# Register reads without assertions, an unrolled run of tiles, and no closing drain in a fused four-layer kernel

## The reference

```python
# layer 0: each sequence takes one of 16 domain experts
idx = jnp.clip(domain_id, 0, E - 1)
Wsel = expert_W[idx]
expert_out = jnp.einsum('bsa,boa->bso', hidden, Wsel) + bsel[:, None, :]
...
# layer 3: each token takes the two likeliest of 8 experts
probs = jax.nn.softmax(h_flat @ router_w, axis=-1)
gates, idx = jax.lax.top_k(probs, TOPK)
gates = gates / gates.sum(-1, keepdims=True)
combine = jnp.zeros((N, E), h_flat.dtype).at[jnp.arange(N)[:, None], idx].add(gates)
hid = jax.nn.relu(jnp.einsum('nd,edf->nef', h_flat, exp_w1) + exp_b1)
eout = jnp.einsum('nef,efd->ned', hid, exp_w2) + exp_b2
y = jnp.einsum('ned,ne->nd', eout, combine)
return x + y.reshape(x.shape)
```

## Time and profile before

| what | value |
|---|---|
| median of 3 runs | 672.55 us (671.54 to 674.32) |
| the profiled execution, own time | 665.42 us |
| its span, first to last instruction | 663.5 us |
| TensorE busy | 580.9 us (88%), 5008 matmuls |
| VectorE, ScalarE, POOL busy | 459.8, 307.0, 221.7 us |
| granted TensorE clock, mean | 0.943 of full speed |
| expert tiles | about 404 us to the end |

### The profile page before, as it was taken

How to read it: one execution, slowest core, us unless ns; L and a number is a source line. 1 busy time by engine, 2 the same in 40 slices (tenths; PEclk the granted TensorE clock), 3 DMA queues, 4 the chain that set the end, 5 groups by cost and what they waited for, 6 DMA issues and landing times.

```text
span 663.5 us, 15716 instructions
## 1 busy us (share of the span) xinstructions
PE 580.9 (88%) x5008; PEld 418.8 (63%) x5009; DVE 459.8 (69%) x1284; ACT 307.0 (46%) x643; POOL 221.7 (33%) x137
## 2 busy tenths in 40 slices
PE   3979989899889979689976899899799999999992
PEld 1537565386665846656656368677667778787771
DVE  6756994899979798654996926877545656564651
ACT  2328357536475254644433234657563434344440
POOL 3141614048225363171530602113532313231322
PEclk9687899999989998889989899999899999999996
DMA  6994019531376332664317758863522322122220
GB/s 205 310 245 166 4 49 238 177 107 42 127 144 207 128 126 68 157 202 179 128 56 259 245 227 302 283 174 91 145 42 42 49 37 42 35 45 43 45 36 0
DMA packets 41177, 86.37 MB, mean 130 GB/s; under 512 B 7321, under 2 KB 31938, under 8 KB 37026
## 3 DMA queue, kind: packets, MB, share of 16 engines
q1 hardware_dynamic: 21248, 56.47, 24.9%
q0 software_dynamic: 8352, 16.99, 13.9%
q10 hardware_dynamic: 11522, 12.20, 6.2%
HBM read 57.10 MB, written 29.44 MB: 130 GB/s over the span
## 4 chain that ended last, share of the span: by engine, by line
PE 49%; DVE 22%; DMA 8%; ACT 8%; issue 6%; ACTq 3%; POOL 2%; SPq 1%; DVEq 0%; POOLq 0%
PE bank L1943 8%; PE bank L1752 6%; PE bank L1932 5%; DMA stage<-in_moe_w 4%; PE bank L1934 4%; PE bank L1933 4%; PE bank L1944 4%; PE bank L1716 2%; ACTq L880 2%; PE bank L1732 2%; DVE split L1024 2%; PE bank L1761 2%; ACT split L684 2%; PE bank L1668 2%; DVE sc_sum L1137 2%
## 5 line engine op out<-in xcount | busy, mean ns | idle before, releaser
L1932 PE MATMUL bank<-xs_f,w_moe 128*128 128x128 f16 x624 | 123.0, 221 | 12.2 <-ACT stage L892 6.3
L892 ACT ACTIVATE stage<-bank,cols 128x128 f32<-128x128 f32 x312 | 88.4, 375 | 78.5 <-issue 30.7
L1934 PE MATMUL bank<-xs_f,w_moe 128*128 128x128 f16 x624 | 123.1, 221 | 0.0
L1933 PE MATMUL bank<-xs_f,w_moe 128*128 128x128 f16 x624 | 122.5, 220 | 0.0
L645 POOL DMA_INDIRECT out_x<-x_kept,ids x39 | 63.2, 1621 | 167.2 <-DVE x_kept L1518 106.7
L1932 PEld LDWEIGHTS bank<-xs_f,w_moe 128*128 x624 | 61.1, 98 | 48.8 <-issue 20.5
L1943 PE MATMUL bank<-w_moe,split 128*128 x208 | 79.2, 383 | 0.5
L1024 DVE SCALAR_TENSOR_TENSOR split<-stage,split 128x2048 f16<-128x2048 f32 x16 | 41.0, 2565 | 34.7 <-ACT split L684 34.6
L1933 PEld LDWEIGHTS bank<-xs_f,w_moe 128*128 x624 | 61.4, 98 | 2.8
L1934 PEld LDWEIGHTS bank<-xs_f,w_moe 128*128 x624 | 61.1, 98 | 1.2
L557 POOL TENSOR_TENSOR w_moe<-w_moe,sc_max 128x2048 f32<-128x2048 f32 x8 | 29.0, 3621 | 97.5 <-DVE sc_max L1132 97.5
(11 more groups left out here) (274 smaller groups left out, 1194.1 us busy)
## 6 DMA issues: line engine op xcount, KB each, us to landing
stage<-in_moe_w SPq DMA_DIRECT2D x16, 1024.0 KB, 7.6
w_split<-split SPq DMA_DIRECT2D x16, 1024.0 KB, 5.0
w_moe<-w_split SPq DMA_DIRECT2D x8, 2048.0 KB, 8.8
w_moe<-in_bias POOLq DMA_DIRECT2D x8, 1024.0 KB, 9.5
xs<-dispatched ACTq DMA_DIRECT2D x41, 130.0 KB, 2.1
w_moe<-in_x_f SPq DMA_DIRECT2D x4, 512.0 KB, 7.0
w_moe<-in_x_t SPq DMA_DIRECT2D x4, 512.0 KB, 12.5
out_x<-x4b ACTq DMA_DIRECT2D x4, 512.0 KB, 3.4
```

Source lines behind the costliest of these rows:

```text
L892: ins = act.activation(h32[j][:, f, :], bank[banks + g][:, P * (f % 4):P * (f % 4) + P], ACT.Relu, bias=moe_b1[:, bass.ds(e, 1), f], scale ...
L1932: pe.matmul(o, hi, xs_f[j][:, k, :], start=(k == 0), stop=False)
L1933: pe.matmul(o, hi, xs_f[j][:, KD + k, :], start=False, stop=False)
L1934: mm = pe.matmul(o, lo, xs_f[j][:, k, :], start=False, stop=(k == KD - 1))
```

## The change

ScalarE no longer reads `tile_ei`: it reads the packed words of `turn_ei`, takes each expert by shift and mask, and reads the row numbers as before; `tile_ei` and the two conversions that wrote it go. All these reads, SP's and ScalarE's reads of the domain experts and TensorE's word reads are built without the range test and the assertion. (SP's read of the row numbers of the regions' ends, line 511, keeps them.) TensorE's tiles 14 to 37 are written out instead of looped, and it reads the word of the next turn before the last of the eight pieces of a turn's last tile, instead of after the tile; the wait for the late plan moves there with it. ScalarE's, VectorE's and POOL's loops stay. The block is built with `no_gpsimd_drain=True`, so POOL's drain at its end is left out.

```diff
--- before.py
+++ after.py
@@ -58,6 +58,7 @@
 LEFT = 2 + TURNS * STEPS
 ENTRIES = LEFT + STEPS
 DIGIT = E
+CLAMPED = "VectorE holds the numbers within their range where it writes them"
...
@@ -304,7 +305,6 @@
...
-        tile_ei = sb("tile_ei", [1, ENTRIES], I32)
...
-        block = ctx.enter_context(nc.Block())
+        block = ctx.enter_context(nc.Block(no_gpsimd_drain=True))
...
@@ -429,7 +429,8 @@
                 sp.wait_ge(dom_ready, 1)
                 sp.wait_ge(w_step.sem, w_step.of(c, 0))
                 _, chosen = nc.values_load_multi_w_load_instructions(
-                    dom_at[0:1, bass.ds(c * CB, last)], engines=[mybir.EngineType.SP], min_val=0, max_val=NDOM - 1)
+                    dom_at[0:1, bass.ds(c * CB, last)], engines=[mybir.EngineType.SP], min_val=0, max_val=NDOM - 1,
+                    skip_runtime_bounds_check_because=CLAMPED)
                 for b in range(last):
                     sp.dma_start(w_raw[:, b, :], t["exp_w"][bass.ds(chosen[b], 1), :, :].rearrange("e a o -> a (e o)")
                                  ).then_inc(w_raw_in.sem, 16)
@@ -793,7 +794,8 @@
             act.wait_ge(dom_ready, 1)
             _, chosen = nc.values_load_multi_w_load_instructions(
-                dom_at[0:1, CB // 2:CB], engines=[mybir.EngineType.Activation], min_val=0, max_val=NDOM - 1)
+                dom_at[0:1, CB // 2:CB], engines=[mybir.EngineType.Activation], min_val=0, max_val=NDOM - 1,
+                skip_runtime_bounds_check_because=CLAMPED)
...
-            def values_of(table, n, count, most):
-                _, values = nc.values_load_multi_w_load_instructions(
-                    table[0:1, bass.ds(n, count)], engines=[mybir.EngineType.Activation], min_val=0, max_val=most)
-                return values
+            def rows_at(n, count):
+                _, rows = nc.values_load_multi_w_load_instructions(
+                    tile_ri[0:1, bass.ds(n, count)], engines=[mybir.EngineType.Activation], min_val=0,
+                    max_val=E * CAP, skip_runtime_bounds_check_because=CLAMPED)
+                return rows
+            def words_of(turn, count):
+                _, words = nc.values_load_multi_w_load_instructions(
+                    turn_ei[0:1, bass.ds(turn, count)], engines=[mybir.EngineType.Activation], min_val=0,
+                    max_val=DIGIT ** (STEPS + 2) - 1, skip_runtime_bounds_check_because=CLAMPED)
+                return words
+            def expert_in(word, j):
+                return (word >> (DIGIT.bit_length() - 1) * j) & (E - 1)
...
             act.wait_ge(plan_ready, 1)
             act.wait_ge(rows_sent.sem, rows_sent.of(NCH - 1, 0))
-            row_at = values_of(tile_ri, 0, 4, E * CAP)
+            row_at = rows_at(0, 4)
             for n in range(2):
                 load_rows(row_at[n], n)
             split_high(NCH - 1, 3)
-            expert = values_of(tile_ei, 0, 4, E - 1)
+            words = words_of(0, EARLY_TURNS)
+            expert = [expert_in(words[0], n) for n in range(4)]
             act.wait_ge(w_out.sem, w_out.of(NCH, 0))
             for n in range(2):
                 act.wait_ge(weights_in, expert[n] * 16 + 16)
@@ -950,8 +965,9 @@
                 high(n, j, n % 3, 1)
             for first in range(2, EARLY - 2, 4):
-                row_at = values_of(tile_ri, first + 2, min(4, EARLY - 4 - first + 2), E * CAP)
-                expert = values_of(tile_ei, first, min(6, EARLY - first), E - 1)
+                row_at = rows_at(first + 2, min(4, EARLY - 4 - first + 2))
+                turn = first // STEPS
+                expert = [expert_in(words[turn], n - turn * STEPS) for n in range(first, min(first + 6, EARLY))]
                 for n in range(first, min(first + 4, EARLY - 2)):
...
             act.wait_ge(plan_ready, 2)
-            row_at = values_of(tile_ri, EARLY, 2, E * CAP)
-            expert = values_of(tile_ei, EARLY - 2, 4, E - 1)
+            row_at = rows_at(EARLY, 2)
+            word, = words_of(EARLY_TURNS, 1)
+            expert = [expert_in(word, n) for n in range(4)]
             for n in range(EARLY - 2, EARLY):
                 early_step(n, row_at[n + 2 - EARLY], expert[n + 4 - EARLY], expert[n + 2 - EARLY])
@@ -974,14 +991,15 @@
                 hidden(n, j, (2 * j + 2) % 4, e, 1)
             with act.Fori(EARLY_TURNS, TURNS) as i:
-                row_at = values_of(tile_ri, i * STEPS + 4, STEPS, E * CAP)
-                expert = values_of(tile_ei, i * STEPS + 2, STEPS + 2, E - 1)
+                row_at = rows_at(i * STEPS + 4, STEPS)
+                now, after = words_of(i, 2)
                 for j in range(STEPS):
-                    late_step(i * STEPS + j + 2, j % 2, row_at[j], expert[j + 2], expert[j])
-            row_at = values_of(tile_ri, LEFT + 2, TILES - LEFT, E * CAP)
-            expert = values_of(tile_ei, LEFT, TILES - LEFT + 2, E - 1)
+                    e_after = expert_in(now, j + 4) if j + 4 < STEPS + 2 else expert_in(after, j + 4 - STEPS)
+                    late_step(i * STEPS + j + 2, j % 2, row_at[j], e_after, expert_in(now, j + 2))
+            row_at = rows_at(LEFT + 2, TILES - LEFT)
+            word, = words_of(TURNS, 1)
             for n in range(LEFT, TILES):
-                late_step(n, n % 2, row_at[n - LEFT], expert[n - LEFT + 2], expert[n - LEFT])
+                late_step(n, n % 2, row_at[n - LEFT], expert_in(word, n - LEFT + 4), expert_in(word, n - LEFT + 2))
...
-                plan_step(dve.tensor_copy(tile_ei[:, 0:EARLY], tile_e[0:1, 0:EARLY]))
...
-                plan_step(dve.tensor_copy(tile_ei[:, late], tile_e[0:1, late]))
...
-            def experts_of(i, count):
-                number = pe.value_load(turn_ei[0:1, bass.ds(i, 1)], min_val=0, max_val=DIGIT ** (STEPS + 2) - 1)
-                return [(number >> (DIGIT.bit_length() - 1) * j) & (E - 1) for j in range(count)]
+            def word_of(turn):
+                return nc.values_load(turn_ei[0:1, turn:turn + 1], engines=[mybir.EngineType.PE], min_val=0,
+                                      max_val=DIGIT ** (STEPS + 2) - 1, skip_runtime_bounds_check_because=CLAMPED)
+            def expert_in(word, j):
+                return (word >> (DIGIT.bit_length() - 1) * j) & (E - 1)
...
-            def early_step(n, e, e_before):
+            def early_step(n, e, e_before, ahead=None):
+                word = None
                 tile_in(n)
                 for f in range(KF):
                     if n > 0 and f % 4 == 0:
@@ -1973,16 +1994,26 @@
                         down(n % 2, (n - 2) % 3, e_before, f)
                     if n > 0 and f == KF // 2:
                         early_turn_rows(n + 1)
-            def late_step(n, j, m, turn, e, e_before):
+                    if ahead is not None and f == KF - 2:
+                        if ahead == EARLY_TURNS:
+                            pe.wait_ge(plan_ready, 2)
+                        word = word_of(ahead)
+                return word
+            def late_step(n, e, e_before, ahead=None):
+                word = None
+                j = n % 2
                 tile_in(n)
                 for f in range(KF):
                     up(j, (2 * j + 2) % 4, e, f)
-                    down(j, (m + 1) % 3, e_before, f)
+                    down(j, (n - 2) % 3, e_before, f)
                     if f == KF // 2:
-                        turn_rows(n + 1, 1 - j, turn, bank[7 - j][:, 0:D])
+                        turn_rows(n + 1, 1 - j, (n + 1) // 2, bank[7 - j][:, 0:D])
+                    if ahead is not None and f == KF - 2:
+                        word = word_of(ahead)
+                return word
...
@@ -1996,15 +2027,17 @@
             pe.wait_ge(xs_f_ready, 1)
             early_turn_rows(1)
             feed_forward2(c, range(3, TT))
+            after = word_of(0)
             for part in range(EARLY_TURNS):
-                experts = experts_of(part, STEPS + 2)
+                word = after
                 if part == 0:
                     for n in range(2):
                         pe.wait_ge(weights_seen, n + 1)
-                        early_step(n, experts[n], None)
+                        early_step(n, expert_in(word, n), None)
                 for j in range(STEPS):
                     n = part * STEPS + j + 2
-                    early_step(n, experts[j + 2], experts[j])
+                    after = early_step(n, expert_in(word, j + 2), expert_in(word, j),
+                                       part + 1 if j == STEPS - 1 else None)
...
-            pe.wait_ge(plan_ready, 2)
-            with pe.Fori(EARLY_TURNS, TURNS) as i:
-                experts = experts_of(i, STEPS + 2)
+            for turn in range(EARLY_TURNS, TURNS):
+                word = after
                 for j in range(STEPS):
-                    late_step(i * STEPS + j + 2, j % 2, (j + 2) % 3, i * (STEPS // 2) + (j + 3) // 2, experts[j + 2],
-                              experts[j])
-            experts = experts_of(TURNS, TILES - LEFT + 2)
```

(6 more changed lines are left out.)

## The result

The changed kernel takes 654.55 us (median of 5 runs, 653.16 to 655.99), the kernel before 672.55 (5 runs beside them, 670.58 to 674.32): a ratio of 0.974, 95% interval 0.9715 to 0.9764. Forecast were 653.0 and a range of 647 to 664.

What follows compares the result with a forecast made beforehand. TensorE, 49% of the chain, bounds the kernel, waiting for ScalarE, its own sequencer and in slow stretches. 5.6 + 1.5 + 5.2 + 0.4 + 0.9 + 5.9 = 19.5 us off the 672.55 median gives 653.0, range 647 to 664.

Steps and rivals of the forecast that it cites:

- Part 1, early tiles: ScalarE's reads before the late loop: dropping assertions and the expert load shrinks TensorE's waits, 5.6 us, bounds 2 to 8.
- the ceiling: Early tiles' upper limit of 7.8 us: TensorE's gaps at four places plus 1.4 us for a clock dip.
- Part 1, the loop's first turn: ScalarE's reads in the late loop: only the first turn shows them, 1.5 us, bounds 0.5 to 2.5.
- Part 2: TensorE's late tiles without a loop: 5.2 us, ends 2 and 8.4, plus 0.4 for turn starts at 455 and 496.
- register operation at its middle: Inside a late turn every tile loses this and its wait's register addition, 0.2 us of sequencer time.
- The word ahead of the last eighth: TensorE's load, 0.36 us, not hidden for certain; by the 64-instruction queue it would cost nothing, some 1.6 us more gain.
- Part 3: SP's range tests ahead of the first chunk's loads, for which POOL waits until 11.15: 0.9 us, bounds 0 to 1.
- Part 4: POOL's closing DRAIN of 5948 ns goes at the span's end: 5.9 us, bounds 0 to 5.95.
- next late: Rival: POOL's chain caps the early gain at 5.6 us at tile 11, or 2.6; 657 us; chance 0.2 with others.
- The drain did not move behind the span: Rival it answers: the runtime waits for POOL behind the span just as long, 659 us; chance 0.12.
- Reading the words is cheaper than reading with assertions: Rival it answers: taking experts from words costs ScalarE as much, part 1 gives 1 us, 659 us; chance 0.08.
- the fetch rival: Unrolled late tiles fetch some 12 more 16 KB blocks, 1.63 us each: 19.6 us, time 672.6; chance 0.06.

Runs made afterwards that it cites:

- The five traces with idle places: Changed kernel twice (654.55, 654.17 us), whole change with TensorE's loop kept (659.46), and both with added empty instructions, dropped at build (653.92, 660.79).
- the nine without: Kernel before (twice), drain left out, ScalarE/SP/VectorE edits (twice), unrolling, assertions dropped with expert table kept, whole change looped with untested word read, changed kernel's last run: 644.85 to 667.58 us.
- third trace: The changed kernel measured once more, without a new edit: 644.85 us against 667.62 for the kernel before, ratio 0.964.
- The words alone: Kernel before with only the ScalarE, SP and VectorE edits (packed words, no range assertions, no expert table): 657.77 us, ratio 0.983; measured again 656.21, 0.981.
- the unrolling: Kernel before with only TensorE's edits (no late loop, words read ahead, no range assertions): 667.47 against 667.74 us; whole change with loop kept 659.46, changed 654.17.
- looped: Whole change with TensorE's late loop kept: with its range assertions 659.46 us, ratio 0.982; with a bare word read 650.88 us, ratio 0.974.
- first trace: Profiled execution of the changed kernel from its first measurement: own time 655.13 us, median 654.55 against 672.55 for the kernel before.

## Why the prediction was right

**The level.** The kernel before took 667.6 to 668.7 us in three series and 672.6 to 673.0 in two. The five traces with idle places in tiles 9 and 10 belong to the two slower ones, the nine without (the profiled execution of before, 665.42 us, counted among them) fit the faster ones. That this execution is of the faster level I take from its time and from the missing idle places; the runs listed with it are of the slower one. If so, it lay 7.1 us under its median because of the level, some 5 us, and because its tile 0 began at 404.00, the earliest of all traces (404.0 to 408.1). The prediction took the sum off the slower median, and missed by 1.6 us. Part of that closeness is luck. The gain was 18.0 and 18.9 us in the two slower series and 22.8 in the faster one, against 19.5 in the sum: the sum is some 3 us short where nothing stalls, and in the slower series the changed kernel loses more to the stall (9.3 to 9.7 us between the levels) than before does (some 5). That the third trace has an own time of 645.82, where 645.9 was worked out for the profiled execution, is luck of the same kind: its expert tiles and closing gained 21.4 us, and its tile 0 began 1.8 us later.

**Point by point**, from before to that third trace, which has none of the idle places; the differences are 3.6, 6.1, 2.9, 2.8 and 6.0 us, less 1.8 us by which tile 0 starts later, 19.6 in all, against 19.5 in the sum:

- *Part 1, early tiles* (5.6 forecast, ceiling 7.8): undersized. The words alone took 7.2 us off tiles 0 to 13, and 9.1 in their second measurement. The step that failed is the ceiling, which counted visible gaps and one clock dip. Tile 7, which begins behind the gap of 447.83, shows what it left out: 7.14 us before, 5.92 with the words, though only one idle place of 0.37 us and one of 0.20 stand in it. Its eighths 4, 5 and 8 take 1.20, 1.09 and 1.35 us, and 0.66, 0.88 and 1.08 with the words: an engine that was late for one tile is late for the next as well. That ScalarE was still catching up there is my reading, not shown by itself. At tile 11 the idle time fell from 3.38 us to 0.42 and the clock dip went, as said (0.6 forecast). The 1.51 us at 424.38 were not won whole: the rows come in time, but at 427.51 TensorE now waits 1.15 us for VectorE's copy of them, which stands in VectorE's order behind 3.3 us of other work (`stats` and `mv`, 422.58 to 426.01); tile 3 fell from 8.05 to 7.08 us.
- *Part 1, the loop's first turn* (1.5): oversized. The words took 0.9 us off; the rest was TensorE's own.
- *Part 2* (5.2 + 0.4): right in sum, incomplete in mechanism. On top of the rest the unrolling brought 5.3 us, and alone nothing that can be measured (0.3 us, interval -0.5 to 2.3). The condition was not in the prediction, which costed the parts one by one and added them: ScalarE's 14 numbers a turn were called hidden, but what hid them was the very pause that part 2 removes. Because part 1 removes them too, the sum stood. Within it the three last turns fell by 2.8 us, not 3.9: a turn takes 34.3 us, 1.2 over six plain tiles of 5.52, where 0.8 was left. The third to fifth tile of a turn are not tighter (5.55 to 5.66 us against 5.53 to 5.71), so the "register operation at its middle" was worth nothing, and the turn's start nearly all: the last eighth before it takes 1.77 to 1.94 us looped and 0.84 to 0.91 unrolled, a plain one 0.66.
- *The word ahead of the last eighth* is not hidden, as the rows of before spoke for: that eighth takes 0.87 us at the median, 0.21 more. The Trainium skill (Advanced Engine Details and Errata, Engine Queue Depths) gives TensorE a queue of 64 instructions. The prediction worked out from it that the 0.3 us load could cost nothing; the trace shows that it did not.
- *Part 3* (0.9): oversized, and not visible in the time. POOL's first work starts at 11.15 to 11.90 us in the four traces with assertions on SP and at 10.79 to 11.43 in the ten without, means 11.56 and 11.04: 0.5 us earlier, with ranges that overlap. In the start of tile 0 nothing of it can be seen: 404.0 to 408.1 us in four traces with assertions on SP, 405.2 to 407.9 in ten without, means 406.5 and 406.4.
- *Part 4* (5.9): 5.8 us by time, 6.0 by trace.

**The rivals.** POOL was not next late for TensorE: its second burst began at 469.72 in the third trace, 1.3 us before tile 11. Counted from tile 0, tile 11 began 6.7 us earlier than before (65.28 against 72.01), where this rival capped the gain at 5.6. VectorE did wait for POOL's confirmations (8.3 us in six places in that trace, up to 2.5), but none of it reached TensorE, whose waits above don't hold an output. The drain did not move behind the span. Reading the words is cheaper than reading with assertions. Of the fetch rival, both halves can be read. In the late turns of the third trace 13 blocks are fetched from 525 to 630 us, one in 8 us, and none of them leaves an idle place over 0.12 us, so a crossing is hidden there. This agrees with the Trainium skill (Runtime: NRT & Kernel Launch, Instruction fetch mechanics), which calls the cost of crossing a 16 KB block mostly hidden. What the prediction named as its sign, new idle places inside late tiles, did not appear. Those that did stand in tiles 9 to 11, with and without unrolled code.

**What stays open** is the cause of those idle places. They reach further than TensorE's "issue" rows say. In the changed kernel's first trace TensorE turned the rows of tile 10 at 464.43 (0.39 us); VectorE, idle for 3.76 us, copied them only at 468.92. In the third trace the same copy starts at 463.42, 0.66 us after the turning began at 462.76 (timelines of VectorE, first and third trace):

```profile
468.92 0.42 DVE L1520 COPY xs_f<-bank 128x512 f16<-128x512 f16 x1 [3.76 <-remote]
...
463.42 0.42 DVE L1520 COPY xs_f<-bank 128x512 f16<-128x512 f16 x1
```

"Remote" is a wait that was ended, but by no instruction or transfer of this core that the profile can name. VectorE has such waits, 2.6 to 10.7 us in all, in each of the five traces with idle places, and no engine has one in the nine without (404 to 490 us). ScalarE has them in four of the five. So VectorE had the turned rows some 4 us late. Whether TensorE finished them late or only its signal came late, the profile doesn't show, since it models the ends of matmuls.

The idle places begin within about a microsecond of POOL's last dispatches of a burst and of the add behind them; in four of the five traces the first begins within 0.1 us of the start of the fourth dispatch, at 465.2 in the changed kernel's first trace (timeline of POOL):

```profile
465.31 0.97 POOL L596 DMA_INDIRECT dispatched<-disp,slot  x1 [0.30 <-issue]
466.59 1.61 POOL L646 DMA_INDIRECT out_x<-x_kept,ids  x1 [0.30 <-issue]
```

but in the third trace the same burst runs with no idle place beside it:

```profile
463.65 0.97 POOL L596 DMA_INDIRECT dispatched<-disp,slot  x1 [0.30 <-issue]
464.93 1.61 POOL L646 DMA_INDIRECT out_x<-x_kept,ids  x1 [0.30 <-issue]
```

So it takes something of the series besides, which the traces don't name; it is not the chip, as said. Nor was a trace of before taken in a slower series, so that its 5 us there come from the same places is likely, not shown. What the change is worth depends on it: 2.6 to 2.8% in the slower series, 3.6% in the faster one.

## What to carry to other kernels

Two engines that pause at the same moment hide each other: over the three later turns the words alone took 0.35 us off, the unrolling alone added 0.8, and both together took off 2.8. So before a step is dropped for bringing nothing, read which wait took the place of the one removed. On ScalarE a register read cost more by its range tests than by its loads here (7.3 of 10 us), so pack numbers into one word, bound them by a mask, and keep tests out of the reading engine's critical stretch. Before a profiled execution is taken as the base of a sum, set it against the median and ask what the 1% between them is; here it was a condition of the series that moved the gain from 18.0 to 22.8 us.

## What the hardware showed unexpectedly

POOL's drain at the block's end took 5.95 us though its last transfer had been confirmed, and could be left out whole. One and the same kernel had idle places of up to 1.8 us on TensorE, put down to its sequencer, between matmuls that waited for nothing, in two series, and none in another: 653.3 and 653.1 against 643.9 us of span, the last two of them on chip number 14. In the same stretches VectorE and ScalarE stood in waits of 2.6 to 6.2 us that the profile puts down to no instruction of the core. A register load's time depends on more than its count: two numbers took 0.49 to 0.51 us, four 0.31 to 0.51, and six, read at the same line of the same loop, 0.75 to 1.34.
